# Half of the decay matrix built from repeated rows on VectorE and ScalarE instead of by a matmul

## The reference

```
A_cumsum = jnp.cumsum(Ac, axis=-1)
L = jnp.exp(segment_sum(Ac))            # L[i,j] = exp(cs_i - cs_j) for j <= i, else 0
Gm = jnp.einsum('bcihn,bcjhn->bhcij', C, B)
Y_diag = jnp.einsum('bhcij,bcjhd->bcihd', Gm * L, xs)
...
states = jnp.einsum('bckhn,bhck,bckhd->bchdn', B, decay_states, xs)
Y_off = jnp.einsum('bckhn,bchdn,bhck->bckhd', C, states, state_decay)
y = (Y_diag + Y_off).reshape(b, l + pad, NH, HD) + D_res
y = y * jax.nn.silu(gate)               # then a norm per group and the output projection
```

## Time and profile before

| | us |
|---|---|
| median of 3 runs | 1945.55 |
| the runs | 1945.05 to 1952.96 |
| the profiled execution | 1945.33 |
| its span in the trace | 1943.6 |
| prologue, until the scan's matmuls start | 265.5 |

### The profile page before, as it was taken

One profiled execution on the slowest core, in us unless ns is written; L12 is line 12 of the kernel. 1 busy time (PEld: TensorE's weight loads), 2 busy tenths in 40 slices (PEclk: granted clock), 3 DMA queues, 4 the chain that ended last, 5 costly groups with the idle time before them and its releaser, 6 DMA issues.

```text
span 1943.6 us, 28857 instructions
## 1 busy us (share of the span) xinstructions
PE 1881.3 (97%) x10416; PEld 1474.4 (76%) x10416; DVE 1450.5 (75%) x1699; ACT 1169.4 (60%) x1907; POOL 949.0 (49%) x692
## 2 busy tenths in 40 slices
PE   6998999999999999999998999999999999999987
PEld 4776777777777777777776777878787878787765
DVE  6876746878777877778785868687878787777776
ACT  3334346777677776767775656666565656566652
POOL 6656643645555455555553444444344444444432
PEclk9999999999999999999999999999999999999999
DMA  2324463455464637463646344342425252424241
GB/s 88 119 82 141 135 218 96 134 169 176 145 190 136 210 131 226 134 207 126 211 129 225 94 134 130 101 137 78 154 83 161 82 161 76 153 75 159 63 131 44
DMA packets 123100, 264.59 MB, mean 136 GB/s; under 512 B 18112, under 2 KB 24384, under 8 KB 122704
## 3 DMA queue, kind: packets, MB, share of 16 engines
q1 hardware_dynamic: 88240, 161.55, 26.4%
q10 hardware_dynamic: 34720, 101.20, 16.2%
HBM read 216.82 MB, written 45.88 MB: 135 GB/s over the span
## 4 chain that ended last, share of the span: by engine, by line
PE 83%; issue 4%; POOL 4%; ACT 3%; DMA 3%; DVE 2%; ACTq 1%; SPq 0%; POOLq 0%; DVEq 0%
PE bank L1069 38%; PE bank L1127 6%; PE bank L1168 5%; PE bank L1184 5%; PE bank L1179 5%; PE bank L1089 5%; PE bank L1102 4%; PE bank L721 3%; PE bank L1134 3%; PE bank L694 3%; PE bank L1114 3%; DMA wlo_scratch<-stage 1%; PE bank L680 1%; POOL wxp L314 1%; POOL ya L1463 1%
## 5 line engine op out<-in xcount | busy, mean ns | idle before, releaser
L1069 PE MATMUL bank<-xnp,wxp 128*128 128x512 f32 x3432 | 861.5, 403 | 10.1 <-POOL wxp L1439 6.3
L1069 PEld LDWEIGHTS bank<-xnp,wxp 128*128 128x128 f32 x3432 | 634.5, 189 | 162.1 <-POOL wxp L1439 15.9
L1439 POOL TENSOR_TENSOR wxp<-wxs,wxp 128x512 fp32r<-128x512 f32 x286 | 382.2, 1339 | 540.1 <-ACT wxp L1296 539.5
L1528 DVE SCALAR_TENSOR_TENSOR conv<-bank,cws,conv 128x509 f32<-128x509 f32 (+2 forms) x480 | 358.0, 746 | 11.3
L1303 ACT ACTIVATE conv<-bank,cbs,cws 128x512 f32<-128x512 f32 x160 | 124.2, 776 | 286.9 <-PE bank L1069 269.3
L1469 POOL TENSOR_TENSOR yl<-gT,yh 128x1024 fp32r<-128x1024 f32 x64 | 156.4, 2444 | 214.2 <-ACT yh L1360 214.2
L1296 ACT ACTIVATE wxp<-wxs 128x512 fp32r<-128x512 f32 x286 | 178.1, 623 | 0.0
L1615 DVE SCALAR_TENSOR_TENSOR M<-M,gb 128x1024 f32<-128x1024 f32 x128 | 171.3, 1339 | 7.5 <-DVE gb L1607 0.5
L1347 ACT ACTIVATE ya<-xT,dch 128x128 f32<-128x128 f32 x512 | 156.2, 391 | 0.0
L1338 ACT ACTIVATE M<-bank 128x1024 f32<-128x1024 f32 x64 | 65.7, 1026 | 138.1 <-PE bank L1134 138.1
L1179 PE MATMUL bank<-wosh,yh 128*128 128x512 f32 x512 | 136.6, 409 | 7.8 <-issue 7.2
(11 more groups left out here) (162 smaller groups left out, 2885.8 us busy)
## 6 DMA issues: line engine op xcount, KB each, us to landing
wxs<-wp SPq DMA_DIRECT2D x288, 256.0 KB, 2.8
wosh<-whi_scratch ACTq DMA_DIRECT2D x64, 512.0 KB, 6.1
wosl<-wlo_scratch ACTq DMA_DIRECT2D x64, 512.0 KB, 11.0
ecs<-ecs_scratch ACTq DMA_DIRECT2D x112, 256.0 KB, 4.5
stage<-wout SPq DMA_DIRECT2D x64, 256.0 KB, 3.0
whi_scratch<-stagh SPq DMA_DIRECT2D x64, 256.0 KB, 2.0
wlo_scratch<-stage SPq DMA_DIRECT2D x64, 256.0 KB, 2.4
wxs<-w SPq DMA_DIRECT2D x56, 256.0 KB, 2.8
```

The lines of the kernel that those rows point to most:

```text
L1069: last = pe.matmul(bank(k), wxp[:, k % 2, a, kk, :], xnp[:, b, kk, :], start=kk == 0 and a + b == 0, stop=kk == KT - 1 and a == 1)
L1439: pool.tensor_tensor(wxp[:, k % 2, 1], wxs[:, k % AHEAD], wxp[:, k % 2, 0], ALU.subtract).then_inc(w_lo, 1)
L1528: last = dve.scalar_tensor_tensor(out=conv[:, n % CB, back:], in0=bank(k)[:, 0:TH - back], scalar=cws[:, g, j, i:i + 1], in1=conv[:, n % C ...
```

## The change

Of the 16 heads of a cell, the first 8 are built another way. The prologue writes the cumulative sums, transposed, to a DRAM tensor `rows_scratch` (one transfer from ACT), and a fourth column of the table `tab` holds -cs_j. In the scan, SP loads for each cell the 8 x 128 sums as one row of 4 KB repeated over all 128 partitions (512 KB) straight into M (`load_sums`), once `diagonal` has read M; DVE's new `bound` computes max(-cs_i, -cs_j) in place; ACT's `exp_a` becomes eight operations of 128x128, exp(-M + bias) with bias -cs_j, so that the exponent is min(cs_i, cs_j) - cs_j. `segment_a` falls away, and the bank X and `segr` serve the other 8 heads alone. `exp_b` takes over the wait for `diagonal(q)`. In ACT's order `exp_a` moves from before `high_y` to after `square`, and `high` of the fifth weight tile ahead (`ks[2] + 2`) moves from behind `exp_b` to before `exp_a`.

```
@@ sync
+            def load_sums(q):
+                if q < CELLS:
+                    _, half, g, c = place(q)
+                    sp.wait_ge(yd_mm, done(q))
+                    sp.dma_start(M[:, 0:HB].rearrange("p h t -> p (h t)"),
+                                 bc(rows_dram[half * CH + c, g, 0:HB].rearrange("h i -> (h i)"), 0, [P, HB * P])
+                                 ).then_inc(d_m, 16)
...
                 for i, k in enumerate(tiles_of(q)):
                     load_tile(k + 2 + AHEAD)
+                    if i == 1:
+                        load_sums(q + 1)
...
+                if not tiles_of(q):
+                    load_sums(q + 1)
@@ tensor
-                if not opens(q):
-                    diagonal(q)
-                    if more:
-                        segment_a(q + 1)
+                if not opens(q):
+                    diagonal(q)
@@ scalar
             def exp_a(q):
-                act.wait_ge(sa_mm, done(q + 1))
-                act.wait_ge(yd_mm, done(q))
-                act.activation(M[:, 0:HG // 2].rearrange("p h t -> p (h t)"), X[:], ACT.Exp).then_inc(e_a, 1)
+                u, _, _, c = place(q)
+                if c == 0:
+                    act.wait_ge(d_tab[u % 2], (u // 2 + 1) * 16 * (1 + PARTS))
+                act.wait_ge(m_min, done(q + 1))
+                for h in range(HB):
+                    last = act.activation(M[:, h], M[:, h], ACT.Exp, scale=-1.0, bias=tab[:, u % 2, 3, c, h:h + 1])
+                last.then_inc(e_a, 1)
...
-                if more:
-                    exp_a(q + 1)
                 high_y(q)
                 square(q)
                 if closes(q):
                     leave_bank(ks[2])
+                else:
+                    for k in ks[2:3]:
+                        high(k + 2)
                 if more:
+                    exp_a(q + 1)
                     exp_b(q + 1)
                 load_row(q + 2)
                 if not closes(q):
                     for k in ks[2:3]:
-                        leave_bank(k)
+                        empty_bank(k)
@@ vector
+            def bound(q):
+                u, _, _, c = place(q)
+                if c == 0:
+                    dve.wait_ge(d_tab[u % 2], (u // 2 + 1) * 16 * (1 + PARTS))
+                dve.wait_ge(d_m, 16 * (q + 1))
+                dve.scalar_tensor_tensor(out=M[:, 0:HB], in0=M[:, 0:HB], scalar=-1.0,
+                                         in1=bc(tab[:, u % 2, 3, c, 0:HB], 2, [P, HB, P]), op0=ALU.mult,
+                                         op1=ALU.max).then_inc(m_min, 1)
...
                 add_diagonal(q)
                 gate(q)
+                if more:
+                    bound(q + 1)
                 for k in ks[2:3]:
                     convolve(k)
```

More of the change, by code:

```diff
@@ L47 @@
 OUTW = 12
-TABS = 3
+TABS = 4
 CREDIT = 8
@@ L52 @@
 PAIRS = P // 2
+HB = HG // 2
 SEG = PAIRS + PARTS * HG
@@ L109, in build @@
         segl = sb(sets, "segl", [ROWS, 2, CH, P], BF16)
-        segr = sb(sets, "segr", [ROWS, HG, P], BF16)
+        segr = sb(sets, "segr", [ROWS, HB, P], BF16)
         d_w = [sem(f"d_w{b}") for b in range(AHEAD)]
@@ L389, in gpsimd @@
                     pool.wait_ge(s_seg, 1)
+                    pool.wait_ge(d_rows, 16)
                     pool.tensor_tensor(flat, flat, csb[:, 0], ALU.subtract).then_inc(s_seg, 1)
@@ L502, in scalar @@
                                            ACT.Exp).then_inc(s_ta, 1)
+                        act.activation(tabs[:, half, :, 3].rearrange("p g c h -> p c g h"),
+                                       cs[:, half * CH:(half + 1) * CH, :].rearrange("p c (g h) -> p c g h", g=G),
+                                       ACT.Copy, scale=-1.0).then_inc(s_ta, 1)
+                if n == PERM + 4:
+                    act.wait_ge(s_trc, NT // 2)
+                    act.dma_start(rows_dram.rearrange("c g h i -> (g h) c i"), csT[:]).then_inc(d_rows, 16)
                 if n == PERM + 8:
@@ L604, in steps_two @@
                     dt_half = dt[:, half * CH:(half + 1) * CH, :].rearrange("p c (g h) -> p c g h", g=G)
-                    dve.wait_ge(s_ta, 2 * half + 2)
+                    dve.wait_ge(s_ta, 3 * half + 3)
                     for c in range(CH):
@@ L860, in scan @@
         built = sem("built")
+        d_m, m_min = sem("d_m"), sem("m_min")
         tap_d, conv_step, conv_d, silu_d, z_d = (
             sem(x) for x in ("tap_d", "conv_step", "conv_d", "silu_d", "z_d"))
-        yo_mm, st_mm, xt_mm, yd_mm, sa_mm, sb_mm, g_mm, o_mm, q_mm = (
-            sem(x) for x in ("yo_mm", "st_mm", "xt_mm", "yd_mm", "sa_mm", "sb_mm", "g_mm", "o_mm", "q_mm"))
+        yo_mm, st_mm, xt_mm, yd_mm, sb_mm, g_mm, o_mm, q_mm = (
+            sem(x) for x in ("yo_mm", "st_mm", "xt_mm", "yd_mm", "sb_mm", "g_mm", "o_mm", "q_mm"))
         e_a, e_b, y_sq, y_hi, y_lo = (sem(x) for x in ("e_a", "e_b", "y_sq", "y_hi", "y_lo"))
@@ L1021, in sync @@
             load_tab(0)
+            sp.wait_ge(d_rows, 16)
+            load_sums(0)
             for k in range(AHEAD + 2, TILES + AHEAD + 2):
@@ L1054, in tensor @@
         def tensor(pe):
-            for s in (yo_mm, st_mm, xt_mm, yd_mm, sa_mm, sb_mm, g_mm, o_mm, q_mm):
+            for s in (yo_mm, st_mm, xt_mm, yd_mm, sb_mm, g_mm, o_mm, q_mm):
                 pe.sem_inc(s, CREDIT)
@@ L1129, in diagonal, with segment_b @@
                 last.then_inc(yd_mm, 1)
-            def segment(q, n):
-                for b in range(2):
-                    head = n * (HG // 2) + b * (HG // 4)
-                    last = pe.matmul(X[:, b * 512:(b + 1) * 512], segl[:, q // CH % 2, q % CH],
-                                     segr[:, head:head + HG // 4, :].rearrange("p h t -> p (h t)"),
-                                     start=True, stop=True)
-                last.then_inc(sb_mm if n else sa_mm, 1)
-            def segment_a(q):
+            def segment_b(q):
                 u, _, _, c = place(q)
@@ L1145, in segment_a @@
                 pe.wait_ge(e_b, done(q))
-                segment(q, 0)
-            def segment_b(q):
-                pe.wait_ge(e_a, done(q + 1))
-                segment(q, 1)
+                for b in range(2):
+                    last = pe.matmul(X[:, b * 512:(b + 1) * 512], segl[:, q // CH % 2, q % CH],
+                                     segr[:, b * (HG // 4):(b + 1) * (HG // 4), :].rearrange("p h t -> p (h t)"),
+                                     start=True, stop=True)
+                last.then_inc(sb_mm, 1)
             def gram(q):
@@ L1195, in tensor @@
             for k in range(TILES):
-                if k == 8:
-                    segment_a(0)
                 if k == 13:
@@ L1317, in leave_bank @@
                     gate(k)
+            def leave_bank(k):
+                empty_bank(k)
                 high(k + 2)
@@ L1331, in exp_a @@
             def exp_a(q):
-                act.wait_ge(sa_mm, done(q + 1))
-                act.wait_ge(yd_mm, done(q))
-                act.activation(M[:, 0:HG // 2].rearrange("p h t -> p (h t)"), X[:], ACT.Exp).then_inc(e_a, 1)
+                u, _, _, c = place(q)
[5 more added lines that the diff above has]
+                last.then_inc(e_a, 1)
             def exp_b(q):
                 act.wait_ge(sb_mm, done(q + 1))
+                act.wait_ge(yd_mm, done(q))
                 act.activation(M[:, HG // 2:].rearrange("p h t -> p (h t)"), X[:], ACT.Exp).then_inc(e_b, 1)
@@ L1508, in vector @@
         def vector(dve):
-            for s in (conv_step, conv_d, s_mul, s_add, u1_d, u3_d, y_d, x_dt, x_dec, g_cp, m_mul, y_s, r_v, acc_d):
+            for s in (conv_step, conv_d, s_mul, s_add, u1_d, u3_d, y_d, x_dt, x_dec, g_cp, m_min, m_mul, y_s, r_v, acc_d):
                 dve.sem_inc(s, CREDIT)
@@ L1640, in vector @@
                 convolve(k)
+                if k == 8:
+                    bound(0)
                 if k == 14:
```

16 lines of the change are left out of this document (9 added, 7 removed).

## The result

| | before | after |
|---|---|---|
| median, us | 1946.67 | 2110.86 |
| lowest of the runs, us | 1945.05 | 2097.84 |
| the profiled execution, its span, us | 1945.33, 1943.6 | 2113.3, 2111.6 |
| mean granted clock of TensorE | 0.997 | 0.963 |
| TensorE, VectorE, ScalarE, GpSimd busy | 97, 75, 60, 49% | 91, 71, 59, 46% |

The ratio is 1.0821 (95% interval 1.0798 to 1.0843): 8.2% slower, where the prediction had 1988 us and 1945 to 2055. One of after's four runs (8813.9 us) was disturbed, and the ratio leaves it out. The direction was right; the forecast increase of 43 us was about a quarter of the measured 164.

What follows compares the result with a forecast made beforehand. TensorE, busy 97%, was taken to bound the kernel. Terms 13.5 + 5.6 + 14 + 11.2 - 2.8 + 1.5 gave 43 us on about 1945: 1988 us, 2.2% slower, eight-in-ten range 1945 to 2055.

Steps and rivals of the forecast that it cites:

- the slot: From diagonal's end to square_sum's start, 14.2 us in a unit's third cell, 13.8 after; all new work hangs there.
- `segment_a`, 0.4 us per cell: Its matmuls' removal gives TensorE 0.4 us per cell, 25.6 us over 64 cells.
- The transfer in an ordinary cell, 4.7 us: SP's load of the 512 KB of rows into M lands 4.7 us after issue, bounds 3.7 and 6.
- rival 1: The transfer lands early, bound starts before low_y and isn't locked out: +12 us, 1958 us; chance 0.15.
- c0, the step that failed: Units' first cells, weights in flight: +14 us for 7 first-half cells, +5.6 for 7 second-half; bounds 0 to +5 per cell.
- c1: Units' second cells, 15: VectorE is late, square_sum waits 1.3 us, net +0.9 each, +13.5 us.
- The table load: ScalarE's 1.28 us table load for the exps carries no wait any more, so it ends before bound does.
- c3 before a fresh cell: Units' fourth cells without from_state in the slot, 7: wait 2.0 us, net +1.6 each, +11.2 us.
- c3 in the second half: Units' fourth cells, 7: low_y is over about 1.3 us earlier, the chain fits, the gain stays: -2.8 us.
- c2 in the first half: Units' third cells, 15 over both halves: wait 0.4 us, gain 0.4, so even, 0 us.
- rival 4: ScalarE's later exp_b delays z's gate and the fourth tile's tap, starving projections: at most some 0.5 us per cell; no chance given.
- Rival 3: The transfer lands late in ordinary cells too, 1 us more in each of some 60: 2048 us; chance 0.23.

Runs made afterwards that it cites:

- b_gain: Kernel before the change, with segment_a's two matmuls of 512 columns replaced by one of 16: 1931.8 us, ratio 0.9932.
- best2_nr: best2 without the reload of the output weights after the first unit: 1955.45 us, 1.0043 to the kernel before.
- hybrid: Sums stay on TensorE in the first half and last unit; only the 28 cells between take the rows as in best2: 1950.61 us, 1.0015.
- best2: Changed kernel, rows loaded a cell ahead, bound directly behind the convolutions, exp_a ahead of high_y without its table wait, high behind exp_b: 1973.8 us, 1.0152.
- norel: Changed kernel with the output weights loaded only for the first unit, no reload: 2023.94 us, 1.0382 to the kernel before.
- b_norel: Kernel before the change, with the output weights loaded only for the first unit: 1943.72 us, 0.9993.
- warm: Changed kernel plus 30 unread transposes on TensorE ahead of square_sum in the first cell of units 1 to 14: 2085.26 us, 1.071.
- notab: Changed kernel without exp_a's own wait for the table tab ahead of each unit's first cell: 2090.08 us, 1.0731.
- norel_notab: Changed kernel with both the edits of norel and notab: 2006.33 us, 1.0298 to the kernel before.

## Why the prediction was wrong, step by step

- What bounds the kernel, and the slot as the place: right. The wait appeared at `square_sum` behind `sum_tiles`, 49 times, 103 us.
- `segment_a`, 0.4 us per cell: nearly right in a cell without other waits, 0.33 to 0.35 (`b_gain`, `best2_nr`), 0.26 to 0.27 with the weights' traffic (`hybrid`, `best2`).
- The transfer in an ordinary cell, 4.7 us: a little too high. The median is 4.7 over all 64, but 4.1 over the 48 cells of the scan outside c0 with the weights (3.5 to 6.3), and 3.5 in the cell shown. There `bound` can start ahead of `low_y` and isn't locked out, as rival 1 had it; where it starts behind `low_y` or the `low` of a tile, it takes up to 3.45 us (mean 1.91, "near 2" was predicted). c2's slots came out even in sum, +2.0 in the first half and -1.7 in the second.
- c0, the step that failed. The prediction said "the landing near +7" and bounded the term by +5 per cell "if it waits for them". The rows land with the weights: in 13 of the 14 cells `bound` starts 9.5 to 13.1 us after `diagonal`'s end (in unit 7, whose slot was 21 us long already, 18.9), and the slots grow by 58 us in place of 20, 4.2 each. So the bound of +5 held, and the value taken from inside it was wrong. I had the row that shows the DMA engines full and used it as a reason for a microsecond or two. The question should have been what is still in flight when the rows are issued, and when it lands. The page of the kernel before has a median for these weights, beside the 3.7 of S that I started from:

```profile
wosl<-wlo_scratch ACTq DMA_DIRECT2D x64, 512.0 KB, 11.0
```

In its trace the last of them lands 7.9 to 10.6 us after `diagonal`'s end in c0 of the second half, and 13.3 to 15.2 in the first (units 1 to 6). For this term the cause is shown: `norel` takes it all away, and `b_norel` shows that the weights alone cost nothing.
- The clock, a term that was missing. Every wait was priced at its own length. After c0's waits TensorE ran at 1.2 GHz for about 7 us, some 2 to 3 us more for each; 33 us are booked in c1 (`warm` removes them and gives back 23 net), and another 11 lie in the first half's c0 outside the slot, behind the waits of the fresh c3. These stay in `norel` (period +10.1, slot -0.9) and go with `notab`, where those waits are shorter (+41.1, +40.5).
- c1: predicted +13.5 in the slot, measured +0.8. The reasoning was right for a kernel whose c0 isn't delayed (+15.5 in `norel`). With c0 delayed and the clock lowered, VectorE catches up, and most of its arrears are gone when c1's `diagonal` starts; in `warm`, with the clock held, the slot has +10.7 again. The term turned into another.
- The table load "carries no wait any more": wrong ahead of the 15 first cells. I generalised from the order of one cell; 21 us with `notab`.
- c3 before a fresh cell, +11.2: +24.0. The table load explains 8 x 1.28 = 10 of it; with `notab` the slots of these cells have +7.4, so some 6 more go with it, which no row assigns.
- c3 in the second half, -2.8: +8.2. The chain doesn't fit there: `bound` takes 1.2 to 2.7 us, and 3.6 us of waits at `square_sum` remain; 6.0 stay in `notab`, mostly outside the slot.
- c2 in the first half, 0: slot nearly right, but the period has +10.7 outside. TensorE waits there 7.8 us for POOL's `low` of a weight tile, which stands behind ScalarE's `high`: close to rival 4. The "8 cells left" of the prediction are 6, which doesn't change its sum. The first cell's +4.4 and the last unit's +12 beyond the forecast are small waits that I didn't follow further.
- The sum by the runs: 164 us over before by the medians, 168 by the spans. 87 are the meeting with the weights and its clock, 18 the table's wait beside it, and 61 stay in `norel_notab`, where the prediction has 43 less 20 for c0, that is 23. So this rest was too low as well, by some 38: by that kernel's periods c2 has +15 in place of 0, the last unit +11 in place of 1.5, the second half's c3 +5 in place of -3, c0 +4. The terms for c1 (+15 for 13.5) and the fresh c3 (+10.6 for 11.2) hold.
- Rival 3, at a chance of 0.23, had the right resource in the wrong cells: not a microsecond more in each of 60, but about five in 14.

The chances were well placed in sign, and the range was too narrow for two reasons: a stretch with full DMA engines, and waits of TensorE behind which every matmul is slower for a while.

## What to carry over

A transfer that must start and land within one cell is priced by what else is in flight in that cell, not by its median: look at the DMA share of the stretch, and where it is 1.0 look up when the transfers in flight land, or count their bytes. A wait of TensorE like those of 3.4 to 3.9 us here costs more than its length, because the clock behind it is lowered; look at an untouched matmul's mean (602 to 714 ns here) for it. And an order is read in each kind of cell: a second wait on one operation moved a table load of 1.28 us into the chain in one cell of four.
